# One run of 32 steps in the cross attention, with norm and turning of x in its first group, and the first weights split in the stage in front

## The reference, cut

```python
    def _L1_xattn_ref(inputs_q, inputs_kv, Wq, Wk, Wv, Wo):
        B, S, D = (8, 256, 512)
        H, HD = (16, 128)
        q = (inputs_q @ Wq).reshape(b, sq, H, HD) * (1.0 / np.sqrt(HD))
        k = (inputs_kv @ Wk).reshape(b, skv, H, HD)
        v = (inputs_kv @ Wv).reshape(b, skv, H, HD)
        scores = jnp.einsum('bqhd,bkhd->bhqk', q, k)
        attn = jax.nn.softmax(scores, axis=-1)
        ctx = jnp.einsum('bhqk,bkhd->bqhd', attn, v).reshape(b, sq, H * HD)
        return ctx @ Wo
    x = x + jnp.tanh(g_xattn[0]) * _L0_xattn_ref(_layernorm(x, axis=-1), ctx_2048, ...)
    x = x + jnp.tanh(g_ffn[0]) * _L0_ffn_ref(_layernorm(x, axis=-1), ...)
    x = x + jnp.tanh(g_xattn[1]) * _L1_xattn_ref(_layernorm(x, axis=-1), ctx_2048, L1_xattn_Wq, L1_xattn_Wk, L1_xattn_Wv, L1_xattn_Wo)
    x = x + jnp.tanh(g_ffn[1]) * _L1_ffn_ref(_layernorm(x, axis=-1), ...)
```

## Time and profile before

| | us |
|---|---|
| runs, median of 3 | 2594.34 (2593.08 to 2594.80) |
| profiled execution | 2599.41 |
| its span, first to last instruction | 2597.6 |
| PE busy | 2253.2 (87%) |
| PEld busy | 1826.7 (70%) |
| DVE busy | 1382.9 (53%) |
| ACT busy | 997.0 (38%) |
| POOL busy | 828.2 (32%) |
| mean granted TensorE clock | 0.941 |

### The profile page before, as it was taken

The page is one execution under the profiler, slowest core; times in us unless marked ns, Lnnn a source line. Parts: engine busy times, 40 slices in busy tenths (PEclk is TensorE's granted clock), DMA queues, the critical chain, the costliest instruction groups (busy, mean ns, idle before and its releaser), DMA issues. The chain is left out here.

```text
span 2597.6 us, 44191 instructions
## 1 busy us (share of the span) xinstructions
PE 2253.2 (87%) x17150; PEld 1826.7 (70%) x17150; DVE 1382.9 (53%) x2420; ACT 997.0 (38%) x1770; POOL 828.2 (32%) x739
## 2 busy tenths in 40 slices
PE   6988996677839999999999998999579998679995
PEld 4666664333428997899878887888467676579995
DVE  7778774677744333433433334333443434477776
ACT  3775342455522222222322222222334443425552
POOL 3332332233303222223322222223434353114543
PEclk8999998899969999999999998999789999889998
DMA  5553102000022001100121112110100000227765
GB/s 227 164 178 100 40 7 95 15 0 0 0 113 82 33 32 71 59 32 32 48 74 33 40 49 74 33 32 25 47 2 2 2 2 2 94 98 261 280 254 219
DMA packets 46750, 191.49 MB, mean 74 GB/s; under 512 B 6928, under 2 KB 6928, under 8 KB 40336
## 3 DMA queue, kind: packets, MB, share of 16 engines
q1 hardware_dynamic: 39568, 166.40, 17.8%
q0 software_dynamic: 7040, 23.07, 2.5%
HBM read 159.04 MB, written 30.41 MB: 73 GB/s over the span
## 5 line engine op out<-in xcount | busy, mean ns | idle before, releaser
L236 POOL TENSOR_TENSOR c_prob<-c_prob,c_inv_mass 128x512 f32<-128x512 f32 x128 | 130.4, 1040 | 392.6 <-DVE c_inv_mass L228 392.6
L218 ACT ACTIVATE c_prob<-c_s_ps,c_neg_peak 128x256 f32<-128x256 f32 x256 | 118.0, 473 | 343.6 <-DVE c_neg_peak L207 343.6
L47 PE MATMUL c_ring<-c_xt_lo,c_w_hi 128*128 128x256 f32 x512 | 149.4, 292 | 21.8 <-DVE c_w_lo L1750 19.2
L1594 POOL TENSOR_TENSOR c_ctx_lo<-c_ctx_f,c_ctx_hi 128x1024 fp32r<-128x1024 f32 x33 | 80.5, 2439 | 271.3 <-ACT c_ctx_hi L1699 271.3
L47 PE MATMUL c_ring<-c_ctx_lo,c_w_hi 128*128 128x256 f32 x512 | 146.4, 286 | 2.1 <-DVE c_qt L1746 2.1
L49 PE MATMUL c_ring<-c_ctx_hi,c_w_lo 128*128 128x256 f32 x512 | 143.8, 281 | 0.0
L49 PE MATMUL c_ring<-c_xt_hi,c_w_lo 128*128 128x256 f32 x512 | 143.8, 281 | 0.0
L48 PE MATMUL c_ring<-c_xt_hi,c_w_hi 128*128 128x256 f32 x512 | 143.7, 281 | 0.0
L48 PE MATMUL c_ring<-c_ctx_hi,c_w_hi 128*128 128x256 f32 x512 | 143.6, 281 | 0.0
L1177 POOL TENSOR_TENSOR b_hw<-b_h,b_lnw 128x512 f32<-128x512 f32 x64 | 80.0, 1268 | 195.9 <-DVE b_h L1342 195.8
L1590 POOL TENSOR_TENSOR c_xt_lo<-c_xt_f,c_xt_hi 128x1024 fp32r<-128x1024 f32 x33 | 84.6, 2564 | 155.0 <-ACT c_xt_hi L1693 155.0
(11 more groups left out here) (518 smaller groups left out, 7143.0 us busy)
## 6 DMA issues: line engine op xcount, KB each, us to landing
x_res<-b_w SPq DMA_DIRECT2D x48, 512.0 KB, 4.9
e_raw<-e_w SPq DMA_DIRECT2D x16, 1536.0 KB, 6.9
c_xt_f<-xnt_scratch SPq DMA_DIRECT2D x33, 512.0 KB, 3.3
c_ctx_f<-ctx_t SPq DMA_DIRECT2D x33, 512.0 KB, 3.4
c_raw<-c_w SPq DMA_DIRECT2D x16, 1024.0 KB, 6.0
h_res<-e_w SPq DMA_DIRECT2D x8, 1536.0 KB, 7.1
wq_scratch<-x_res SPq DMA_DIRECT2D x24, 256.0 KB, 2.7
ab_wq<-wq_scratch SPq DMA_DIRECT2D x3, 2048.0 KB, 12.4
```

What stands on the lines that cost most here:

```text
L47: pe.matmul(out, lhs[0], rhs[1], start=first, stop=False)
L218: ins = act.activation(self.prob[:, u % 2, j, 0:w], self.s_ps[:, j, 0:w], ACT.Exp, bias=self.neg_peak[:, u % 2, j:j + 1], scale=self.scale ...
L236: pool.tensor_tensor(part, part, self.inv_mass[:, u % 2, js].unsqueeze(2).to_broadcast([P, 2, w]), ALU.mult).then_inc(self.prob_done, 1)
L1594: pool.tensor_tensor(ctx_lo[:, :, :], ctx_f[:, :, :], f32(ctx_hi[:, :, :]), ALU.subtract).then_inc(ctx_lo_done, 1)
```

## The change

The first part of the cross attention is gone as a block of its own. In the FFN, SP loads Wq and Wk of the first group at the start, and in the last pair, where no x is left to quantise, DVE takes the statistics of the first four tiles and norms the first two; ACT and POOL split Wq. The tiles for that (`CrossHanded`, names with bc_) live through both stages. The cross attention is one sequence of 32 turns with one turn -1 in front, written out without loops. Turn s makes the fronts of sample s+1 whatever group it belongs to, and in the first group PE also turns x of sample s+2, through the same ring, between front 4 and the weighted sum; ACT copies it to xt_f, from where it is used at once and stored for the later groups. DVE takes the statistics of the last 12 tiles between the copies of turn -1. The weights of a group are split in turns around its start: WQ and WK two turns ahead (`group_after`), WV one ahead, WO in its first turn. The numbers of the ring's uses are found by a dictionary (`use_of`), and each bank has a semaphore of its own for being free.

```diff
@@ -1110,7 +1110,7 @@
-def quantised_ffn(nc, x_res, ident, begun, handed, ln_row, gate):
+def quantised_ffn(nc, x_res, ident, begun, handed, ln_row, gate, cross, cross_w):
...
+        cross_in, cross_hi_done, cross_stats = sem("cross_in"), sem("cross_hi_done"), sem("cross_stats")
...
@@ -1165,6 +1166,9 @@
         def _(sp):
             sp.dma_start(gate_sb[:, :], gate).then_inc(gate_in, 16)
             sp.dma_start(lnw[:, :], ln_row).then_inc(lnw_in, 16)
+            for n in range(2):
+                sp.dma_start(cross.raw[:, n], cross_w[0, n]).then_inc(cross_in, 16)
+            sp.wait_ge(cross_in, 32)
...
@@ -1182,6 +1186,8 @@
             with pool.Fori(1, PAIRS) as i:
                 for par in range(2):
                     weight(i * 2 + par, par)
+            pool.wait_ge(cross_hi_done, 1)
+            pool.tensor_tensor(cross.wq_lo[:, :, :], cross.raw[:, 0], f32(cross.wq_hi[:, :, :]), ALU.subtract)
...
                 if not last:
                     round_x(i + 1)
                     copy_x(i + 1, False)
+                else:
+                    act.wait_ge(cross_in, 32)
+                    act.activation(cross.wq_hi[:, :, :], cross.raw[:, 0], ACT.Copy).then_inc(cross_hi_done, 1)
...
                     add_to_x(i * 2 - 1, 1)
                 if not last:
                     quantise_x(i + 1)
+                else:
+                    for n in range(2 * TB):
+                        cross.tile_stats(dve, x_res, n).then_inc(cross_stats, 1)
+                    dve.wait_ge(cross_stats, 2 * TB)
+                    cross.find_spread(dve, chain, 0, 2 * TB)
+                    cross.normalise(dve, x_res, 0)
                 up(i, 1)
...
+class CrossHanded:
...
+    def tile_stats(self, dve, x_res, n):
+        return dve.bn_stats(self.stats[:, n, :], x_res[:, n, :])
+
+    def find_spread(self, dve, chain, first, end):
+
+        part = slice(first, end)
+        for n in range(first, end):
+            ins = dve.bn_aggr(self.agg[:, n, :], self.stats[:, n, :])
+        chain.step(ins)
+        chain.wait()
+        chain.step(dve.tensor_scalar(self.var[:, part], self.agg[:, part, 1], LN_EPS, None, ALU.add))
+        chain.wait()
+        inverse_sqrt(dve, chain, self.rstd[:, part], self.var[:, part], self.tmp[:, part])
+        chain.wait()
...
+    def normalise(self, dve, x_res, s):
+        for t in range(TB):
+            n = s * TB + t
+            ins = dve.tensor_scalar(self.xn[:, t, :], x_res[:, n, :], self.agg[:, n, 0:1], self.rstd[:, n:n + 1], ALU.subtract, ALU.mult)
+        return ins
...
+def cross_attention(nc, x_res, ident, begun, handed, xnt_dram, ctx_t, w_t, gate):
...
-            norm(0, 0)
-            norm(1, 1)
-            with dve.Fori(1, BATCH // 2) as i:
-                for par in range(2):
-                    norm(i * 2 + par, par)
...
+    STEPS = GROUPS * BATCH
+    WQ, WK, WV, WO = range(4)
...
-        def turns(eng, head, turn):
-
-            def group(g, end):
-                head(g)
-                with eng.Fori(0, BATCH // 2 - 1) as i:
-                    for par in range(2):
-                        turn(g, i * 2 + par, par, False, False)
-                turn(g, BATCH - 2, 0, False, False)
-                turn(g, BATCH - 1, 1, True, end)
-
-            with eng.Fori(0, GROUPS - 1) as g:
-                group(g, False)
-            group(GROUPS - 1, True)
...
+        use_of = {("xt0", 0): 0, ("xt1", 0): 1}
+        for s in TURNS:
+            for name, ahead in (("f0", 1), ("f1", 1), ("f2", 1), ("f3", 1), ("f4", 1), ("xt0", 2), ("xt1", 2), ("f5", 1), ("o0", 0), ("o1", 0)):
+                if turned(s + ahead) if name in ("xt0", "xt1") else here(s + ahead):
+                    use_of[name, s + ahead] = len(use_of)
...
+            def load_weights(g, n):
+                m = 4 * g + n
+                if m > 2:
+                    sp.wait_ge(w_lo_done, m - 2)
+                sp.dma_start(raw[:, n % 2], w_t[g, n]).then_inc(w_in[n % 2], 16)
...
+            def store_turned(s):
+                await_free(sp, "xt0", s)
+                await_free(sp, "xt1", s)
+                sp.dma_start(xnt_dram[s], xt_f[:, :, :]).then_inc(stored, 16)
...
+            def load_inputs(s):
+                if s >= BATCH:
+                    sp.wait_ge(xt_lo_done, s)
+                    if s == BATCH:
+                        sp.wait_ge(stored, 16 * BATCH)
+                    sp.dma_start(xt_f[:, :, :], xnt_dram[s % BATCH]).then_inc(xt_in, 16)
+                if s > 0:
+                    sp.wait_ge(ctx_lo_done, s)
+                sp.dma_start(ctx_f[:, :, :], ctx_t[s % BATCH]).then_inc(ctx_in, 16)
+
+            load_inputs(0)
+            load_weights(0, WV)
...
+            load_weights(0, WO)
+            for s in range(1, STEPS):
+                if turned(s - 1):
+                    store_turned(s - 1)
+                load_inputs(s)
+                g, b = divmod(s, BATCH)
+                if b == 3 and g + 1 < GROUPS:
+                    load_weights(g + 1, WQ)
+                    load_weights(g + 1, WK)
+                if b == 0:
+                    load_weights(g, WV)
+                if b == 1 and g > 0:
+                    load_weights(g, WO)
...
+            def use(name, s, emit):
+                n = use_of[name, s]
+                if n >= 2:
+                    pe.wait_ge(ring_free[n % 2], n // 2)
+                emit(ring[:, n % 2, :]).then_inc(ring_ready, 1)
...
+            def turn_x(s, t):
+                if s > 0:
+                    pe.wait_ge(xn_done, s)
+
+                def emit(bank):
+                    for c in range(C):
+                        mm = pe.transpose(bank[:, c * P:(c + 1) * P], xn[:, t, c * P:(c + 1) * P], ident[:, :])
+                    return mm
+                use(f"xt{t}", s, emit)
+
...
+            turn_x(0, 0)
+            turn_x(0, 1)
+            for s in TURNS:
+                now, nxt = here(s), here(s + 1)
+                if now:
+                    scores(s, 0)
+                if nxt:
+                    queries(s + 1, 0)
+                    queries(s + 1, 1)
+                if now:
+                    scores(s, 1)
+                    att.turn(pe, s, 0)
+                if nxt:
+                    keys(s + 1, 0)
+                    keys(s + 1, 1)
+                if now:
+                    att.turn(pe, s, 1)
+                if nxt:
+                    values(s + 1, 0)
+                if turned(s + 2):
+                    turn_x(s + 2, 0)
+                    turn_x(s + 2, 1)
+                if now:
+                    weigh(s)
+                if nxt:
+                    values(s + 1, 1)
+                if now:
+                    await_weights(s, WO)
+                    pe.wait_ge(att.o_lo_done, s + 1)
+                    for t in range(TB):
+                        use(f"o{t}", s, tokens((w_hi[WO], w_lo[WO]), o_hi, o_lo, t))
...
+            def copy_inputs(s):
+
+                for t in range(TB):
+                    await_ready(act, f"xt{t}", s)
+                    if t == 0 and s > 0:
+                        act.wait_ge(xt_lo_done, s)
+                        act.wait_ge(stored, 16 * s)
+                    act.activation(xt_f[:, :, t * P:(t + 1) * P], chunks(bank_of(f"xt{t}", s)), ACT.Copy).then_inc(free_of(f"xt{t}", s), 1)
...
+            weights_high(0, WK)
+            copy_inputs(0)
+            inputs_high(0)
+            context_high(0)
+            for s in TURNS:
+                now = here(s)
+                if now:
+                    att.exponentials(act, s, 0)
+                if here(s + 1) and (s + 1) % BATCH == 0:
+                    weights_high((s + 1) // BATCH, WV)
+                if now and s % BATCH == 0:
+                    weights_high(s // BATCH, WO)
+                if s == -1:
+                    act.wait_ge(gate_in, 16)
+                    act.activation(gain[:, :], gate_sb[:, :], ACT.Tanh).then_inc(gain_done, 1)
+                if now:
+                    att.exponentials(act, s, 1)
+                if group_after(s) is not None:
+                    weights_high(group_after(s), WQ)
+                if now:
+                    att.copy_turned(act, s, 0, 1, s % 2)
+                    att.copy_turned(act, s, 1, 1, s % 2)
+                if turned(s + 2):
+                    copy_inputs(s + 2)
+                if here(s + 2):
+                    inputs_high(s + 2)
+                if now:
+                    if s > 0:
+                        await_ready(act, "o1", s - 1)
+                    att.output_high(act, s, 0, o_hi[:, :, :], att.o_ps[:, :, :].rearrange("p k (j q) -> p (k j) q", j=2))
+                if here(s + 2):
+                    context_high(s + 2)
+                if group_after(s) is not None:
+                    weights_high(group_after(s), WK)
...
+            def late_stats(k):
+
+                for n in (2 * TB + 2 * k, 2 * TB + 2 * k + 1):
```

(63 more changed lines are left out.)

359 lines of the change are left out of this document (109 added, 250 removed).

## The result

| | before | changed kernel |
|---|---|---|
| runs, median | 2594.57 us (4 runs, 2593.08 to 2597.27) | 2528.99 us (4 runs, 2527.54 to 2529.78) |
| profiled execution | 2599.41 us | 2527.54 us |
| its span | 2597.6 us | 2525.8 us |
| mean granted TensorE clock | 0.941 | 0.952 |

The ratio is 0.9745, 95% interval 0.9729 to 0.9762: 65.6 us faster by the medians, 71.8 by the two profiled spans. The forecast was 2520 us, range 2508 to 2538. The time lies in the range, 9 us above the forecast.

A forecast was written before the change was run, and what follows sets the result against it. TensorE, busy 87% of the span, was taken as the bound, with gaps at group ends and stage front. Terms -49.3+0.9-40.4+7-2.9+4.0+6.8 = -73.9 us, taken from the 2594.34 us median, gave 2520 us, range 2508 to 2538.

The forecast's parts named there:

- Group ends: Three seams between head groups: 47.6 us each become one turn of 31.18, 49.3 us saved.
- The 0.9 us allowed for WK: Seams: WK's low half on DVE delays x additions that free the ring; 0.3 us for each of three, bounds 0 and 3.
- the saving is eaten at the seams: Rival, 15%: weight splits under running turns stop PE, and FFN and turn 0 cost their upper bounds; 2541 us.
- Front of the stage: Last FFN addition to first cross-attention product: 48.60 us become 8.2, 40.4 us saved.
- The rival in which it doesn't shrink: Front rival, 5%: next block starts later, DMAs bring ctx and WV late, DVE's statistics hold copies; 2530 us.
- The FFN: FFN's last pair: DVE's added statistics and norm, plus a slower clock, cost +7 us, bounds +4 and +9.
- an FFN end later by 10 us or more: A sign that would show the forecast wrong, against the predicted last addition 7 us later.
- the insertion: FFN's last pair: statistics, roots and norm on DVE before tile 15's first h, 6.2 us; PE stands about 5.
- First fronts: Turn -1, first product to first scores: 20.8 us instead of 23.7, 2.9 saved; bounds 18.1 and 24.
- Turn 0: First turn: x's transposes, DVE's late peak and Exp table load make 35.2 us instead of 31.2; bounds +1.4 and +8.
- Turns 1 to 5: Each carries 0.8 us of transposes and a 0.55 us bank wait: 1.36 a turn, 6.8 for five; bounds 4 and 10.
- Clock and code: Rivals: clock falls in each of turns 0 to 5, 2551 us (4%); PE waits for code fetches, 2616 us (3%).

The follow-up runs named there:

- wk_twice: Changed kernel with DVE's subtraction for WK's low part done twice at the head groups' seams; one run of 2532.70 us.
- pool_late: Changed kernel with POOL's subtraction for WQ's low part moved from the FFN's last tiles to the start of the cross attention; 2522.76 us (0.9724).
- preload_last: Changed kernel with a one-column exponential ahead of turn 0, its column declared last, POOL not held back; single run of 2521.28 us.
- turn0: Changed kernel with a one-column exponential ahead of turn 0 and POOL's split of turn 1's context held until turn 1's x is normalised; single run of 2530.16 us.
- xt_apart: Changed kernel with the turning of x's second tile, and ACT's copies with it, moved behind the weighted sum in turns 0 to 5; 2522.42 us (0.9730).
- before_again: The kernel before, unchanged, profiled once more; one run of 2594.21 us, span 2592.5.

## Why the prediction was right, and what it missed

**Group ends: right.** 47.6 us became 31.19, and PE doesn't wait in the 25 turns that hold the seams. The 0.9 us allowed for WK were not needed; wk_twice gives the room as 0.45 us. The rival "the saving is eaten at the seams" fell in the changed kernel.

**Front of the stage: right.** 7.43 us against 8.2, by the links that were named. The rival in which it doesn't shrink fell.

**The FFN: right in sign, the term too small.** 8.8 us in the one profile and 10.2 in five others against 7, with bounds of 4 and 9. The usual value is above the upper bound, and "an FFN end later by 10 us or more" was one of the signs of being wrong. The working had the insertion (6.0 measured, 6.2 said; PE stood 3.20 for it and not 5), but took the clock for the second cost, 2 us. Of the split of WQ it said that it "ends before the tile-15 chain of roots, rounding, turning and product does", and gave it no price in the sum. It did end before them. But POOL's part began 0.16 us behind the first operation of the roots and stopped DVE for 4.1 us, as pool_late shows, and all the rest of that chain came later. The mechanism stood only in the upper bound. The clock, put at 2 us, was 0.84 in the first profile against 0.85 before, and its last 16 products took 4.47 us against 5.67 before; it made the 1.4 us between this profile and the others, whose last products took 5.7 us as before.

**First fronts:** 21.55 against 20.8. **Turn 0: too small.** 37.0 against 35.2, inside the bounds. The load of the table was forecast and is worth 1.3 us (preload_last). What was not costed is DVE's 2.25 us beside POOL, and turn0 shows that they can't be had by moving POOL a little. **Turns 1 to 5:** 32.70 against 32.54, by the predicted wait at the predicted place; xt_apart splits the 1.51 us into 0.86 and 0.65 where 0.81 and 0.55 were said.

**Clock and code: fell.** The clock is 1.00 from turn 0 to turn 30, with the transposes in turns 0 to 5. The instruction queue has 131 packets, against 104 and 95 in the two profiles of the kernel before, and the 32 turns written out run at 31.19 us where a turn of the loop took 31.17 (the first of a group 31.27). By the sizes that the Trainium skill gives (Advanced Engine Details and Errata, ISA Cache), PE's code of this run is larger than its cache and has to be fetched; no wait on PE answers to it.

**The median was taken from the wrong execution.** The terms add up to -73.9 us and the profiled spans differ by 71.8. The medians differ by 65.6. The forecast took the sum, made on an execution of 2599.41 us, from a median 5.1 us lower as if that execution's surplus stayed in the changed kernel. A good part of it was in what the change removes: 2.4 us in the 32 turns, by before_again. Against that second profile of before the group ends are worth 46.8 us and not 49.2, and all stretches together 66.7. The 8.6 us between 2520.4 and 2529.0 are then 2.1 us of terms (FFN +1.8, turns +1.6, fronts +0.8, front of the stage -0.8, the stretches outside -1.2), 5.1 us by which before's profiled execution lay above the median that the forecast started from, and 1.5 us by which the profiled execution of the changed kernel lay below its own. That the terms miss by no more than 2.1 us is in part luck: the profile happens to have the FFN's cheapest end of six, and 2.0 us of misses the one way stand against 4.2 the other.

## What to carry to other kernels

Take the price of a stage boundary from PE's busy and idle time there, and ask what part of it is clock: that part changes from one execution to the next, so it wants two profiles before it goes into a sum. Work moved "into a wait" of DVE or POOL has to be laid against the other one's instructions too: here a long subtraction on POOL turned operations of 1 to 12 columns on DVE into ones that last until it ends, and moving it by 3.5 us only changed which one was hit. A serial insertion of 6 us belongs behind the last thing that others wait for, and here moving it there gave back all but about 1 us of the FFN's loss, once POOL was out of the way.

## What the runs showed of the hardware

- DVE operations on 1, 12 and 2 columns took 4.30, 2.25 and 1.87 us (0.16 and 0.17 otherwise) beside a subtraction of 2048 or 1024 columns on POOL, and ended within 0.05 us of it. A subtraction on POOL took 3.37 us instead of 2.37 when DVE's was there first. An operation with one input from SBUF and one column, 0.03 us behind POOL's start, took its usual 0.15 us; but bc_var (12 columns) and c_neg_peak (2 columns), with one input too, were stopped.
- A tile of 4 bytes a partition, declared ahead of others, made products of x with WQ take 283 ns instead of 280 and a turn 31.27 us instead of 31.19.
- Two executions of the kernel before, with the same idle time at a group end (9.6 us), differed by 2.76 us there: the clock was 0.86 in one and 0.92 in the other.
- 32 turns written out, 192 products and as many loads each, ran within 0.02 us a turn of the loop of two turns, with PE never waiting from turn 6 to turn 30.
